# ScalarE gathers half of every other tile's last row block in both layers of a two-layer graph network, and the last pair's results get rows of their own

## What is computed

```python
x = layernorm(x + L0(x, W1, W2, b0, src, dst))
x = layernorm(x + L1(x, W, b1, src, dst))

def L0(feat, W1, W2, b, src, dst):              # deg = max(out_degree, 1)
    msg = (t1[src] + feat[src] * feat[dst] @ W2) / (sqrt(deg[src]) * sqrt(deg[dst]))   # t1 = feat @ W1
    embed = where(in_count > 0, t1 + segment_sum(msg, dst), 0) + b
    embed = leaky_relu(embed, 0.01)
    return embed / max(norm(embed), 1e-12)      # row norm: one square root
def L1(x, W, b, src, dst):
    return segment_sum((x @ W.T + b)[src], dst) / (in_degree + 1)
```

## Time and profile before

| | us |
|---|---|
| median of 3 runs (lowest, highest) | 3892.88 (3892.51, 3895.84) |
| the profiled execution, its own time | 3895.48 |
| span of that execution, first to last instruction | 3893.4 |
| layer 0's gathers, first to last start | 372.4 to 1949.9 |
| layer 1's gathers, first to last start | 1975.5 to 3873.3 |

### The profile page before, as it was taken

The page is one execution under the profiler, slowest core; times in us unless marked ns, Lnnn a source line. Parts: engine busy times, 40 slices in busy tenths (PEclk is TensorE's granted clock), DMA queues, the critical chain, the costliest instruction groups (busy, mean ns, idle before and its releaser), DMA issues.

```text
span 3893.4 us, 62898 instructions
## 1 busy us (share of the span) xinstructions
PE 2701.5 (69%) x10186; PEld 1887.0 (48%) x10186; DVE 1914.7 (49%) x3812; ACT 502.6 (13%) x1540; POOL 2903.2 (75%) x3066
## 2 busy tenths in 40 slices
PE   4551777676766676767767777777777777777777
PEld 4440556565655565656634444444444444444443
DVE  9995466566666666666632333333333333333333
ACT  8992000000000000000000000000000000000000
POOL 7776777777777777777757777777777777777776
PEclk5555888888888888888877777777767777777777
DMA  7878455555555555555534444444444444444443
GB/s 252 271 240 318 144 164 163 163 165 163 164 163 164 161 165 162 162 162 164 150 90 122 127 124 127 122 128 123 127 122 128 122 127 122 127 123 127 121 128 106
DMA packets 322785, 594.32 MB, mean 153 GB/s; under 512 B 71073, under 2 KB 207062, under 8 KB 322582
## 3 DMA queue, kind: packets, MB, share of 16 engines
q0 software_dynamic: 146208, 399.44, 36.3%
q1 hardware_dynamic: 149938, 171.30, 13.4%
q10 hardware_dynamic: 26436, 21.80, 1.8%
HBM read 506.29 MB, written 75.48 MB: 149 GB/s over the span
## 4 chain that ended last, share of the span: by engine, by line
POOL 39%; SPq 21%; issue 21%; DMA 3%; PE 2%; DVE 2%; ACTq 1%; DVEq 1%; POOLq 0%; ACT 0%
POOL ring L589 39%; SPq L464 15%; SPq L457 4%; PE banks L1343 2%; DMA ring<-x,idx 1%; ACTq L767 1%; DVEq L874 1%; SPq L391 1%; SPq L386 1%; DMA x_t<-in_x 1%; SPq L437 1%; SPq L444 0%; PE banks L1311 0%; SPq L472 0%; ACTq L744 0%
## 5 line engine op out<-in xcount | busy, mean ns | idle before, releaser
L1343 PE MATMUL banks<-ring,hot_space 128*128 128x257 f32 x6252 | 2083.6, 474 | 594.4 <-DMA ring<-x,idx 459.9
L1343 PEld LDWEIGHTS banks<-ring,hot_space 128*128 128x128 f32 x6252 | 1308.0, 229 | 1294.9 <-DMA ring<-x,idx 873.1
L589 POOL DMA_INDIRECT ring<-x,idx x1517 | 1436.2, 947 | 487.2 <-issue 457.6
L589 POOL DMA_INDIRECT ring<-scaled_x,idx x1247 | 1192.8, 957 | 396.4 <-issue 381.1
L1050 DVE SCALAR_TENSOR_TENSOR big<-banks,here_mask,big 128x257 f32 x784 | 343.3, 479 | 1415.0 <-PE banks L1343 1409.1
L996 DVE TENSOR_TENSOR hot_space<-banks,dst_rel 128x1024 f32<-128x1024 f32 x345 | 422.0, 1224 | 167.1 <-issue 165.4
L1300 PE MATMUL banks<-ident,halves 128*128 128x128 f32 x588 | 147.1, 413 | 412.2 <-DVE halves L1064 410.2
L1300 PEld LDWEIGHTS banks<-ident,halves 128*128 128x128 f32 x588 | 112.0, 215 | 454.7 <-DVE halves L1064 404.6
L600 POOL DMA_INDIRECT ring<-in_x,src_col x276 | 263.9, 956 | 84.1 <-issue 84.1
L665 ACT ACTIVATE dst_rel<-columns,halves 128x128 bf16<-128x128 f32 x960 | 268.3, 373 | 5.2 <-DVE halves L909 5.2
L704 ACT COPY idx<-src_col 128x32 int32 (+1 forms) x97 | 21.1, 218 | 1570.0 <-issue 774.6
(11 more groups left out here) (122 smaller groups left out, 1171.6 us busy)
## 6 DMA issues: line engine op xcount, KB each, us to landing
src_lo<-scaled_x SPq DMA_DIRECT2D x2944, 1.0 KB
src_lo<-x ACTq DMA_DIRECT2D x2944, 1.0 KB
src_lo<-x SPq DMA_DIRECT2D x2944, 1.0 KB
kept_rows<-ring SPq DMA_DIRECT2D x94, 384.0 KB, 3.3
ring<-kept_rows SPq DMA_DIRECT2D x47, 768.0 KB
ring<-x,idx POOLq DMA_INDIRECT x1517, 4.1
src_lo<-scaled_x ACTq DMA_DIRECT2D x1408, 1.0 KB
ring<-scaled_x,idx POOLq DMA_INDIRECT x1247, 3.3
```

Source lines behind the costliest of these rows:

```text
L589: g.indirect_dma_start(ring[:, u, 0:D], None, table[layer], bass.IndirectOffsetOnAxis(ap=idx[:, idx_buf(layer, n), u:u + 1], axis=0)).then ...
L1343: last = nc.tensor.matmul(group_sum(k % SUMS), dst_hot[:, k % HOTS, u - k * GT, :], ring[:, u, 0:DW], start=u == tiles[0], stop=u == tiles ...
```

## The change

- `ACT_BLOCKS`, ScalarE's `round_` and its loops: ScalarE gathers tile 31 of all odd rounds from 3 to 47 in layer 0 too, 64 rows a round as in layer 1. Its loop in layer 0 now takes two rounds instead of four.
- GpSimd gathers no tile 31 in rounds 3, 7, ... 47 of layer 0: 12 gathers fewer. TensorE's waits and loop follow.
- The blocks of rows stand elsewhere in ScalarE's order, in both layers. Odd rounds (half 0): 32 rows after the clearing (or `take_sums`), 32 after `take_turned`; `pass_hand` now comes after the roots. Even rounds (half 1): 8 before `next_idx`, 24 after the roots, 16 before `take_turned`, 16 behind it.
- The last pair's results go into rows of their own (`out_last`, in `dst_col`), and its `finish_sums` no longer waits for `stored`. Pair 47 is finished inside the last round (in layer 1 wholly, in layer 0 up to its squares), with ScalarE's matching roots moved there.

```diff
-FEW = SPANS
-ACT_BLOCKS = (((0, 16), None, None, (16, 32)), ((0, 24), (24, 32), (32, 48), (48, 64)))
+ACT_BLOCKS = ((0, 8), (8, 32), (32, 48), (48, 64))
...
+        out_last = [dst_col[:, n * D:(n + 1) * D] for n in range(2)]
...
                     for i in range(2, SPAN):
-                        gather_round(layer, i, i, HAND_U if layer or i % 2 == 0 else U, first)
+                        gather_round(layer, i, i, HAND_U, first)
                     with g.Fori(1, SPANS + 1) as h:
                         for n in range(SPAN):
-                            gather_round(layer, SPAN * h + n, n, HAND_U if layer or n < SPAN - 1 else U, first)
+                            gather_round(layer, SPAN * h + n, n, HAND_U, first)
...
                 if hand is not None:
-                    if share == 0:
+                    if half == 0:
                         hand_loaded(layer, hand)
-                    starts = load_starts(layer, hand, share * parts, load_next and parts == 1)
-                if passed is not None:
-                    pass_hand(layer, passed)
-                if hand is not None:
-                    if share == 0:
-                        hand_free(layer, hand)
+                    starts = load_starts(layer, hand, 2 * half, False)
+                if hand is not None and half == 1:
                     hand_block(layer, first_row, 0, starts)
                 if not (last and layer):
                     next_idx(layer, i, n)
                 if ended:
                     roots(layer, i - 2)
-                if hand is not None and parts == 2:
+                if passed is not None:
+                    pass_hand(layer, passed)
+                if hand is not None and half == 1:
                     hand_block(layer, first_row, 1, starts)
                 if sums and layer == 0 and not last:
                     clear_sums(i - 1)
                 if sums and layer == 1:
                     act.wait_ge(groups_added, group_no(layer, i, LAST_K + 1) + SUMS)
                     take_sums(i - 1, acc[:, bass.ds(2 * i - 2, 2), :])
-                if hand is not None and parts == 2:
-                    starts = load_starts(layer, hand, share * parts + 1, load_next)
+                if hand is not None and half == 0:
+                    hand_free(layer, hand)
+                    hand_block(layer, first_row, 0, starts)
+                    hand_block(layer, first_row, 1, starts)
+                if hand is not None and half == 1:
+                    starts = load_starts(layer, hand, 2 * half + 1, load_next)
                     hand_block(layer, first_row, 2, starts)
                 if sums:
                     take_turned(layer, i - 1)
+                if last and layer == 0:
+                    norm_root(i - 1)
+                elif last:
+                    var_root(layer, i - 1)
+                if hand is not None and half == 0:
+                    starts = load_starts(layer, hand, 2 * half + 1, load_next)
+                    hand_block(layer, first_row, 2, starts)
                 if hand is not None:
                     hand_block(layer, first_row, 3, starts)
...
-            def finish_sums(layer, m, sums, xs=x_now, mask=scal, results=project):
-
-                for s in range(2):
-                    v.wait_ge(stored[s], 16 * (node_no(layer, m) + 1))
+            def finish_sums(layer, m, sums, xs=x_now, mask=scal, results=project, rows=out_now):
+
+                if rows is out_now:
+                    for s in range(2):
+                        v.wait_ge(stored[s], 16 * (node_no(layer, m) + 1))
...
+                    if last and k == LAST_K:
+                        norm(layer, i - 2)
+                        finish_sums(layer, i - 1, acc[:, NW - 4:NW - 2, :])
+                        if layer == 1:
+                            moments(layer, i - 1)
+                            norm(layer, i - 1)
```

More of the change, by code:

```diff
@@ L173, in gnn @@
         out_t = [sb(f"out_t{n}", [P, D]) for n in range(2)]
+        out_now = [out_t[n][:, :] for n in range(2)]
         sums_space = sb("sums_space", [P, KEPT * NW])
@@ L308, in act_hand_no @@
         def act_hand_no(layer, h):
-            return layer * FEW + h
+            return layer * HANDS + h
         def one_row(layer, start):
@@ L523, in _ @@
                     for s in range(2):
-                        store(layer, ROUNDS - 1, NW - 2 + s, s)
+                        store(layer, ROUNDS - 1, NW - 2 + s, s, out_last)
                     layer_end(layer)
@@ L727, in take_turned, with norm_root, var_root @@
                                    turned[s][:, 0:parts * D]).then_inc(a_ready[s], 1)
+            def norm_root(m):
+                act.wait_ge(square_ready, m + 1)
+                nc.scalar.activation(pair[2], pair[1], ACT.Sqrt).then_inc(norm_ready, 1)
+            def var_root(layer, m):
+                act.wait_ge(var_ready, node_no(layer, m) + 1)
+                nc.scalar.activation(pair[3], mv[:, :, 1], ACT.Sqrt, bias=epsilon[:, 0:1]).then_inc(var_rooted, 1)
             def roots(layer, m):
                 if layer == 0:
[L731 to L734, removed]
+                    norm_root(m)
+                var_root(layer, m)
             def load_hand_src(layer, h):
-                i = 2 * h + 1 if layer else SPAN * h + 1
+                i = 2 * h + 1
                 nc.scalar.dma_start(hand_src[1], row_bytes[bass.ds(i, 1), :]).then_inc(hand_src_in[1], 16)
@@ L762, in hand_block @@
             def hand_block(layer, first_row, block, starts):
-                first, end = ACT_BLOCKS[layer][block]
+                first, end = ACT_BLOCKS[block]
                 for n in range(first, end):
@@ L849, in _ @@
                     take_turned(layer, ENDS)
-                    roots(layer, ENDS - 1)
                     if layer == 0:
+                        var_root(layer, ENDS - 1)
                         for m in range(ENDS - 1, ROUNDS):
@@ L1082, in finish_sums @@
                     for s in range(2):
-                        nc.vector.tensor_tensor_reduce(out=out_t[s][:, :], in0=e[s][:, :], in1=e[s][:, :], scale=1.0,
+                        nc.vector.tensor_tensor_reduce(out=rows[s], in0=e[s][:, :], in1=e[s][:, :], scale=1.0,
                                                        scalar=0.0, op0=ALU.mult, op1=ALU.add,
@@ L1118, in moments @@
                 for s in range(2):
-                    nc.vector.bn_stats(stats[:, s, :], out_t[s][:, :])
+                    nc.vector.bn_stats(stats[:, s, :], rows[s])
                 ordered()
@@ L1124, in moments, with norm @@
                 v.sem_inc(var_ready, 1)
-            def norm(layer, m):
+            def norm(layer, m, rows=out_now):
                 v.wait_ge(var_rooted, node_no(layer, m) + 1)
@@ L1154, in round_ @@
                         moments(layer, i - 2)
-                    if ended and k == LAST_K:
+                    if ended and k == LAST_K and not last:
                         norm(layer, i - 2)
```

78 lines of the change are left out of this document (28 added, 50 removed).

## The result

| | before | after |
|---|---|---|
| time, median | 3893.25 us (3892.51 to 3895.84) | 4197.25 us (4193.25 to 4199.43) |
| ratio, 95% interval | | 1.0773 [1.0761, 1.0786] |
| span of the profiled execution | 3893.4 us | 4197.6 us |
| period of layer 0, clearing of pair 4 to that of pair 44, / 20 | 64.5 us | 78.5 us |
| clearing to root of an even pair | 17.5 us | 32.0 us |

The forecast was 4129 us with a range of 4072 to 4215. The direction, the place and the mechanism came as forecast; the time lies 68 us above the forecast, next to rival A's 4186. The range held it because it took in rival A.

The account below looks back on a forecast made before the run. SyncE's queue was taken to pace layer 0, with GpSimd nearly as full, and GpSimd layer 1. 3895.5 + 240 (late roots) - 3.5 (last pair's rows) = 4132 us, median 2.6 lower: 4129 us, range 4072 to 4215.

Parts of the forecast that it names:

- rival A: Layer 0: ScalarE's branch back at the loop's end stalls as before, 57 us more, 4186 us; chance 0.13.
- The root, K + 29.0: Layer 0: ScalarE reaches the even pair's root 29.0 us behind K, that pair's clearing, instead of 17.9, 11.1 us late.
- The loop's end: ScalarE's branch back in layer 0: priced at about nothing as in layer 1, though layer 0 showed 2.77 us standing still.
- Root to store, store to x, x to clearing: Layer 0, even pair's root to SyncE's store 8.9 us, to the next even x load 33.5, to the next clearing 4.9.
- second ring: Layer 0's wait loop, clearing to clearing through both roots without SyncE: reaches K + 71, before the 75.6 us SyncE needs.
- first ring: Layer 0's wait loop through ScalarE's even root and SyncE's store and x load: period from 64.5 to about 75.6 us.
- The odd pair, "no charge": Layer 0, even to odd round: odd root reached 16.5 us behind its clearing, before VectorE's 17.6; products 2.7 late, no cost.
- The sum: Layer 0's loss: 7 us for pair 2, 222 for 20 periods of 11.1, 11 for pair 44, together 240 us.
- Layer 1 and the tail: Layer 1: the new order costs 0; at the kernel's end the last pair's own rows save 3.5 us.
- B: Layer 0: ScalarE keeps up and SyncE still paces; 3875 to 3889 us, 3885 likely; chance 0.09.
- C: Layer 0: only the late copies and products count, 4.7 us a period, 99 us, 3988 us; chance 0.06.
- D: Layer 0: denser issue, 0.34 us a row, 72 rows cost 2 us more, 44 us, 4173 us; chance 0.08.

Follow-up runs that it names:

- experiments 8 to 10: 11 GpSimd gathers left out of the kernel before, 3889.42 us; SyncE's code moved by 110 instructions on `e4`, 3887.00 us; both together, 3879.80 us.
- e4: The kernel before with only the last pair's own result rows and pair 47's end inside the last round: 3887.30 us, 0.9985.
- experiment 6: The changed kernel with ScalarE's code moved by 75 semaphore increments ahead of layer 0: 4140.84 us, 1.0638.
- experiment 7: The changed kernel with 32 of SyncE's 128 rows left out of each period of layer 0: 4135.23 us, 1.0616.
- experiment 11: The kernel of experiment 7 with the odd pair's copies to a_t ahead of its load and 16 rows: 4066.19 us, 1.0448.
- experiment 3: The changed kernel with the same rows, loads and gathers of ScalarE's layer 0 in another order around the roots: 3996.83 us, 1.0269.
- experiment 5: The changed kernel with the copies to a_t behind 8 of the 32 rows in odd rounds of layer 0: 4200.83 us, 1.0791.
- experiment 9: `e4` with SyncE's code moved by 110 and by 200 instructions ahead of layer 0: 3887.00 us (0.9980) and 3888.68 us (0.9983).

## Why the prediction came out as it did

**What bounds.** "SyncE's queue paces layer 0" was half of it. The chain of waits names one engine; "GpSimd is nearly as full" was the other half, and experiments 8 to 10 show that the two stood within about 1 us a period (64.3 us in `e4`, 63.9 with SyncE relieved, 63.3 with both). For this change it made no difference, since ScalarE became later than both.

**The root, K + 29.0.** Measured 32.0. Without the stall it is 29.3 (experiment 6). The terms held: 32 rows and the step 10.9 us instead of 10.3; from the copies to the index copy 21.1 us, of which 2.7 are the stall, and 18.4 remain where 18.5 stood.

**The loop's end.** This is the step that failed: "My sum takes the layer 1 price since the new body is like layer 1's". A like body is no guide, as experiment 6 shows with the same body at another place. Rival A had the right mechanism and 57 us; moving the code brought 56 and moving the loop's end 61. A at 0.13 was too low: the trace had a stall in one of two loops, and nothing in it told which the new body would be. The Trainium skill ("Runtime: NRT & Kernel Launch", Instruction fetch mechanics) says that a taken branch stalls for a fetch when its target is outside the two pages of instructions held at the time. The traces agree in kind: the same body has a gap of 2.46 us when it begins 303 instructions from the program's start and of 0.24 at 378, and a shorter body lost SyncE's gap at an unchanged start. They don't show which places are outside.

**Root to store, store to x, x to clearing.** 8.9, 33.5 and 4.9 us in the prediction; 8.9, about 33.1 (32.5 to 33.6 in 19 of the 20 periods) and about 4.6 in the trace. The first ring was right term by term, and so was the price of 1 us a period for each us of a late root, down to the second ring.

**The odd pair, "no charge".** Right in its result, narrow in its reason. I put the second ring at K + 71, 4.6 us before the first. It takes 75.5 us (experiment 7) against 78.5, so 3.0 us before it. Both have the stall in them; without it the first takes 75.8, and the second would take about 72.8 (an estimate: 75.5 less 2.7). So it was 1.8 us longer than I had it. I had 20.3 us at most from clearing to root of the odd pair (17.6 + 2.7); it takes 20.3 to 22.3 with the copies 8 us late, and 17.2 with the copies in time (experiment 11).

**The sum.** 240 us were forecast in layer 0, 304 came. For the 20 periods, 222 were forecast and 279 measured ((78.48 - 64.51) x 20). Of these 57 us the stall is (78.48 - 75.75) x 20 = 55. Pairs 2 and 44 cost 10.6 and 11.7 us instead of 7 and 11, the first again the stall. Another 2.5 us stand ahead of pair 2, where I had nothing.

**Layer 1 and the tail.** Layer 1 takes 1901.9 us from its first to its last gather and took 1897.7; the kernels with the old order of layer 1 lie at 1897.7 to 1903.5, those with the new one at 1899.6 to 1901.9, so the order costs nothing there. The last pair's results start 0.04 us behind the products instead of 3.52, as forecast; from the last gather to the end of the span it is 17.6 us and was 20.1. Experiment 4 measured 5 [2 to 9] us; in the changed kernel the gain is hidden in the 4.2 us by which that execution's gathers took longer.

**The rivals.** A came true. B fell: ScalarE was late by 14 us, and in the better order of experiment 3 the period is still 3.3 us longer than before. C fell in experiment 5. D: 32 rows took 10.5 us, 0.33 a row, which makes 10.9 us with the steps instead of 10.3, but 24 rows took 7.36 us, 0.31 a row; it holds for some tenths of a us a period and not for 2.

## What to carry to other kernels

When rows or other cheap work of an in-order queue are set between the chain's own steps, write down every ring that passes through that engine, from one event to the same event a period later, and price each; relief in one ring ends at the next (here 78.5 us, then 75.5 to 76.8, then 72, and before the change two queues within about 1 us). Work that doesn't fit between two roots in one order may nearly fit in another: the same 128 rows cost 304 us here and 104 there, some 60 of the difference being the stall. And look at each loop's branch for a gap: where it stands on the chain, moving the loop's end or the code changes the time for nothing, and an edit of the body may switch it on or off, in that loop and in those behind it in the program.

## What the runs showed of the hardware

**The stall at a branch back goes with the place of the code and, as it seems, its length.** ScalarE's bodies of 303 to 306 instructions stalled when they began at 303, 444, 924, 925 or 1210 from the program's start and didn't at 378, 995 or 1000; SyncE's of 312 stalled at 423 and not at 533 or 623, and one of 247 didn't at 423. The instruction queue's packets count the stalls: 352 in the changed kernel, 143 with both of ScalarE's loops free of them, 5 packets for each of the 42 branches, 8.2 KB each; and 188 in the kernel before, 88 with SyncE's 20 stalls gone (experiment 9), 5 each again. Which places are good ones the runs don't settle.

**Products behind a longer wait ran slower.** Two stretches of TensorE in the changed kernel, an even pair's and an odd pair's products:

```profile
1304.55 6.58 PE L1320 MATMUL banks<-w_s,a_t 128*128 128x256 f32 x16 [5.65 <-ACT a_t L727]
...
1345.76 3.72 PE L1320 MATMUL banks<-w_s,a_t 128*128 128x256 f32 x16 [2.94 <-ACT a_t L727]
```

The granted clock in these two stretches, for the most part at 1.2 and wholly at 2.4 GHz (columns: us, busy us of PE, PEld, DVE, ACT, POOL, then the clock):

```profile
1304.50:1311.20 6.70, 6.65 (x18) 5.33 (x19) 0.00 (x0) 0.49 (x1) 4.32 (x5) 0.56 0.44 117
1345.70:1349.40 3.70, 3.64 (x17) 3.23 (x18) 2.49 (x4) 0.49 (x2) 2.79 (x4) 1.00 0.54 152
```

After 5.65 us of standing still the same 16 matmuls took 6.58 us instead of 3.72. In experiment 5, where the copies come in time and the products follow without a wait, those of the even pair take 3.62 us. It costs nothing here, since the root behind them waits for ScalarE's rows (experiment 5, with the products in time, has the same period).
